# A decoder layer on one core: scaled B and C tiles laid out by batch, sums of squares in four column groups

## The reference

```python
bc = jnp.einsum('bti,oi->bto', value, W_bc).reshape(Bsz, Tlen, H, 4, N)      # H = 32 heads, N = 32 states
bc = bc / (jnp.sqrt(jnp.sum(bc * bc, axis=-1, keepdims=True)) + EPS)
Bz, Bx, Cz, Cx = (bc[..., i, :] for i in range(4))
def step(carry, inp):
    z, s = carry
    S = 1.0 / (1.0 + dt * k + dt * dt * A)
    z = S * (z - dt * A * s + dt * (Bz * u))
    s = s + dt * z + dt * (Bx * u)
    y = einsum('bhn,bhnd->bhd', Cz, z) + einsum('bhn,bhnd->bhd', Cx, s)
_, ys = jax.lax.scan(step, init, inputs_by_time)
y = (ys + skip * value) * silu(gate);  return y @ W_out.T
```

## Time and profile before

| | us |
|---|---|
| median of 3 runs | 3355.25 (3353.84 to 3386.32) |
| the profiled execution: time, and its span | 3354.0, 3352.2 |
| PE busy | 2969.5 (89%) |
| DVE busy | 2062.2 (62%) |
| ACT busy | 1303.7 (39%) |
| mean granted TensorE clock | 0.927 of full speed |

### The profile page before, as it was taken

The page is one execution under the profiler, slowest core; times in us unless marked ns, Lnnn a source line. Parts: engine busy times, 40 slices in busy tenths (PEclk is TensorE's granted clock), DMA queues, the critical chain, the costliest instruction groups (busy, mean ns, idle before and its releaser), DMA issues. The chain is left out here.

```text
span 3352.2 us, 84244 instructions
## 1 busy us (share of the span) xinstructions
PE 2969.5 (89%) x34360; PEld 2215.4 (66%) x34360; DVE 2062.2 (62%) x7109; ACT 1303.7 (39%) x2246; POOL 287.1 (9%) x227
## 2 busy tenths in 40 slices
PE   5885799999999999999999998698699389999997
PEld 2344577777787777878778776333376156888886
DVE  5445898989989999999988996455533000111110
ACT  3443345444544455444544552233221011333332
POOL 0000000000000000000000000000002710343433
PEclk9887899999999999999999998799859589999998
DMA  6556332444254324443344322200041211777777
GB/s 226 151 157 172 85 95 64 127 102 97 68 122 115 101 79 97 117 110 88 74 127 102 96 63 69 72 1 1 28 203 60 96 46 35 186 202 202 202 206 216
DMA packets 333204, 373.98 MB, mean 112 GB/s; under 512 B 62254, under 2 KB 294848, under 8 KB 328128
## 3 DMA queue, kind: packets, MB, share of 16 engines
q1 hardware_dynamic: 310400, 340.20, 36.5%
q0 software_dynamic: 22464, 28.95, 4.3%
HBM read 269.17 MB, written 104.04 MB: 111 GB/s over the span
## 5 line engine op out<-in xcount | busy, mean ns | idle before, releaser
L605 PE MATMUL ring<-valt,wbc 128*128 128x256 f32 x4096 | 943.4, 386 | 29.9 <-DMA valt<-valt_scratch 27.6
L605 PEld LDWEIGHTS ring<-valt,wbc 128*128 128x128 f32 x4096 | 772.6, 193 | 166.6 <-issue 61.1
L758 ACT COPY bc<-ring 128x512 f32<-128x512 f32 x256 | 149.6, 584 | 732.4 <-PE ring L605 732.3
L918 DVE TENSOR_TENSOR uu<-phi,coef 128x64 f32<-128x64 f32 x2048 | 359.2, 215 | 2.1
L924 DVE TENSOR_TENSOR phi<-phi,uu 128x64 f32<-128x64 f32 x2048 | 358.9, 215 | 0.0
L2023 DVE TENSOR_SCALAR f_yr<-fp_y,f_meta 128x256 f32<-128x256 f32 x124 | 54.3, 479 | 415.2 <-PE fp_y L1839 415.2
L663 PE MATMUL yp<-bc,hpad 32*32 32x64 f32 x8192 | 260.3, 289 | 3.3 <-DVE hc L1024 2.5
L663 PEld LDWEIGHTS yp<-bc,hpad 32*32 32x32 f32 x8192 | 225.3, 121 | 54.2 <-issue 54.0
L1901 ACT ACTIVATE f_hT<-fp_h,f_b 128x256 f32<-128x256 f32 x248 | 117.6, 474 | 328.2 <-PE fp_h L1830 328.2
L1839 PE MATMUL fp_y<-f_w,f_hT 128*128 128x256 f32 x992 | 230.7, 386 | 7.9
L1712 POOL DMA_INDIRECT acc_scratch<-f_yr,f_meta x124 | 192.6, 1553 | 444.3 <-DVE f_yr L2023 276.4
(11 more groups left out here) (226 smaller groups left out, 4168.6 us busy)
## 6 DMA issues: line engine op xcount, KB each, us to landing
f_w<-in_W_dram SPq DMA_DIRECT2D x128, 512.0 KB
coef<-par_scratch SPq DMA_DIRECT2D x128, 256.0 KB, 5.8
fb<-fac_scratch SPq DMA_DIRECT2D x512, 64.0 KB, 2.2
fc<-fac_scratch SPq DMA_DIRECT2D x512, 64.0 KB, 2.6
xg_scratch<-f_fill SPq DMA_DIRECT2D x16, 1032.0 KB, 17.1
f_xr<-xg_scratch SPq DMA_DIRECT2D x64, 258.0 KB
vtok_scratch<-p_vtok SPq DMA_DIRECT2D x32, 512.0 KB, 7.1
dub<-vtok_scratch SPq DMA_DIRECT2D x16, 1024.0 KB, 5.5
```

Of the source, the lines that this page charges most:

```text
L605: mm = pe.matmul(ring[:, p % 2, v * UT:(v + 1) * UT], wbc[:, k, g, first + v, :], valt[:, u % 2, k, :], start=(k == 0), stop=(k == 3))
L758: nc.scalar.copy(bc[:, gp, first:first + 2, i // 2, :], o).then_inc(bc_ready, 1)
L918: made[k] = mark(V.tensor_tensor(uu[:, k].rearrange("p i (g b) -> p i g b", b=B), phi[:, t, ::-1, k, :].rearrange("p i (g b) -> p i g b", ...
```

## The change

`sq` gets two halves, and PE adds the squares of two parts at a time: `summed` runs twice a pass in place of four times, with four program matmuls in the column groups 0 to 3 in place of two. ACT's `Square` of a part waits for the sums of two parts back, no longer for the last one. The last operations of `inputs` and `read_out` write `bc` by batch (column b*128 + i*64 + t over both halves i), reading their sources with a step of 4 elements. PE's three readers of the scaled tiles now read contiguous columns. Since the new layout of one half covers old columns of the other, both writes wait for the last of the products before them (`need(other[1])`).

```diff
-        sq = sb("sq", [P, 2, UT])
+        sq = sb("sq", [P, 2, 2, UT])
+        def batches(v):
+            return v.rearrange("p (t b) -> p b t", b=B)
+        def flat(gp, c):
+            return bc[:, gp, c].rearrange("p i t -> p (i t)")
+        def late(v):
+            return v.rearrange("p (b i t) -> p i b t", b=B, i=2)
...
-            def summed(u, gp, i):
+            def summed(u, gp, half):
...
-                for v in range(2):
-                    c = first + v
-                    mm = pe.matmul(ssp[H * c:H * c + H, 0:UT], sel[:, g, :], sq[:, v, :],
-                                   start=(i < 2), stop=(i >= 2))
+                for i in range(2):
+                    for v in range(2):
+                        c = 2 * i + v
+                        mm = pe.matmul(ssp[H * c:H * c + H, 0:UT], sel[:, g, :], sq[:, i, v, :],
+                                       start=(half == 0), stop=(half == 1))
...
                         mm = pe.transpose(kp[:, v, b * P:(b + 1) * P],
-                                          turns(bc[:, gp, v].rearrange("p i t -> p (i t)"))[:, :, b], ident[:])
+                                          flat(gp, v)[:, b * P:(b + 1) * P], ident[:])
...
                                 mm = pe.matmul(kp[L * i:L * i + L, j, b * L:(b + 1) * L],
-                                               turns(bc[r, gp, v, i, :])[:, :, b],
-                                               turns(bc[r, gp, 2 + v, i, :])[:, :, b],
+                                               flat(gp, v)[r, b * P + i * L:b * P + (i + 1) * L],
+                                               flat(gp, 2 + v)[r, b * P + i * L:b * P + (i + 1) * L],
...
                                 pe.matmul(yp[r, b * L:(b + 1) * L], hpad[r, v, i, b, :],
-                                          turns(bc[r, gp, 2 + v, i, :])[:, :, b],
+                                          flat(gp, 2 + v)[r, b * P + i * L:b * P + (i + 1) * L],
...
-                if p > 0:
-                    act.wait_ge(sums_done, p)
-                nc.scalar.activation(sq[:], o, ACT.Square).then_inc(sq_ready, 1)
+                if p >= 2:
+                    act.wait_ge(sums_done, p // 2)
+                nc.scalar.activation(sq[:, p % 2], o, ACT.Square).then_inc(sq_ready, 1)
...
                 for i, m in enumerate((m1, m2)):
-                    need(other[i])
-                    V.tensor_tensor(bc[:, gp, 0, i, :], fb[:, i, 1, :], m[:, 1, :], ALU.subtract)
-                    ins = V.tensor_tensor(bc[:, gp, 1, i, :], m[:, 0, :], fb[:, i, 0, :], ALU.subtract)
+                    need(other[1])
+                    V.tensor_tensor(late(flat(gp, 0))[:, i], batches(fb[:, i, 1, :]), batches(m[:, 1, :]), ALU.subtract)
+                    ins = V.tensor_tensor(late(flat(gp, 1))[:, i], batches(m[:, 0, :]), batches(fb[:, i, 0, :]),
+                                          ALU.subtract)
...
                 for i, m in enumerate((m1, m2)):
-                    need(other[i])
-                    ins = V.tensor_tensor(bc[:, gp, 2:4, i, :], fc[:, i], m[:], ALU.add)
+                    need(other[1])
+                    ins = V.tensor_tensor(bc[:, gp, 2:4].rearrange("p c i t -> p c (i t)")
+                                          .rearrange("p c (b i t) -> p i c b t", b=B, i=2)[:, i],
+                                          fc[:, i].rearrange("p c (t b) -> p c b t", b=B),
+                                          m[:].rearrange("p c (t b) -> p c b t", b=B), ALU.add)
```

More of the change, by code:

```diff
@@ L607, in projected @@
                 mm.then_inc(ring_full, 1)
-            def summed(u, gp, i):
+            def summed(u, gp, half):
                 n = GP * u + gp
[L612 to L615, removed]
+                g = 2 * gp + half
+                pe.wait_ge(sq_ready, 4 * n + 2 * half + 2)
+                if half == 0 and n > 0:
                     pe.wait_ge(nr_root, n)
-                for v in range(2):
-                    c = first + v
-                    mm = pe.matmul(ssp[H * c:H * c + H, 0:UT], sel[:, g, :], sq[:, v, :],
-                                   start=(i < 2), stop=(i >= 2))
+                for i in range(2):
[3 more added lines that the diff above has]
+                                       start=(half == 0), stop=(half == 1))
                 mm.then_inc(sums_done, 1)
@@ L663, in mixed_states @@
                                 pe.matmul(yp[r, b * L:(b + 1) * L], hpad[r, v, i, b, :],
-                                          turns(bc[r, gp, 2 + v, i, :])[:, :, b],
+                                          flat(gp, 2 + v)[r, b * P + i * L:b * P + (i + 1) * L],
                                           start=(b == 0 and i == 0 and v == 0), stop=False, skip_group_check=True)
                     if b == 0 and more:
-                        summed(un, gn, 3)
+                        summed(un, gn, 1)
                 for v in range(2):
@@ L699, in _ @@
                     projected(0, gp, i)
-                    if gp > 0 or i > 0:
-                        summed(0, gp - (i == 0), (i - 1) % 4)
-            summed(0, GP - 2, 3)
+                    if i == 2:
+                        summed(0, gp, 0)
+                    elif i == 0 and gp > 0:
+                        summed(0, gp - 1, 1)
+            summed(0, GP - 2, 1)
             for u in range(NU):
@@ L710, in _ @@
                         projected(un, gn, 1)
-                        summed(un, gn, 0)
                     if gp == 0 and u > 0:
@@ L716, in _ @@
                         projected(un, gn, 2)
-                        summed(un, gn, 1)
+                        summed(un, gn, 0)
                         projected(un, gn, 3)
-                        summed(un, gn, 2)
                     mixed_states(u, gp, more, un, gn)
@@ L758, in projected @@
                 nc.scalar.copy(bc[:, gp, first:first + 2, i // 2, :], o).then_inc(bc_ready, 1)
-                if p > 0:
-                    act.wait_ge(sums_done, p)
-                nc.scalar.activation(sq[:], o, ACT.Square).then_inc(sq_ready, 1)
+                if p >= 2:
+                    act.wait_ge(sums_done, p // 2)
+                nc.scalar.activation(sq[:, p % 2], o, ACT.Square).then_inc(sq_ready, 1)
             def norms(u, gp):
                 n = GP * u + gp
-                act.wait_ge(sums_done, 4 * n + 4)
+                act.wait_ge(sums_done, 2 * n + 2)
                 if n > 0:
```

## The result

The changed kernel takes 3429.41 us (median of 4 runs, 3420.26 to 3435.87); the kernel before, beside it, 3357.35. The ratio is 1.0193, 95% interval 1.0132 to 1.0255: 72 us, 2%, slower. The profiled execution took 3420.3 us, 66 more than that of before. Its last residual add starts at 2167.3 us in place of 2096.6, so 70.6 us came in up to the end of the mixer and 4 went behind it, where nothing was changed. From the first residual add to the last but one, 14 chunks take 114.3 us each, before 109.7.

A forecast was written before the change was run, and what follows sets the result against it. The prediction took DVE's own loop, not PE, as the bound: 100 us for stepped reads plus 13 for new waits, less 13, 7, 3.5 and 4, gives 85 us on 3354.0, so 3439 us; range 3385 to 3525.

The forecast's parts named there:

- What bounds the kernel: Mixer: DVE's own loop sets the chunk of 108.5 us, not PE, though PE is busy 96%.
- the two waits: DVE's waits for fb in each chunk, 2.67 and 4.81 us, made by DVE's own loop through SP and DMA.
- DVE's price: The stepped reads in inputs and read_out cost DVE 0.76 ns a column more, 1.56 us a pass, 100 us.
- the two rows that met at 1.8: PE's stepped read and ACT's stepped copy, both 1.8 ns a column, taken as the memory's price for DVE too.
- rival 2: DVE's stepped reads: penalties of both sources add, 1.52 ns a column, time 3522 us; chance 12%.
- rival 1: DVE's stepped reads are free, only the new waits add, time 3357 us; chance 12%.
- The 41 us for 1.4 ns: Low end of the forecast's own range: half the step penalty on DVE, 41 us slower, 3395 us.
- The exposed waits: New waits for the product right ahead in inputs and read_out: 0.10 us each, 13 us in all.
- What the waits swallow: DVE's fb waits hide part of its added work: 13 us in the first, 7 us in the second.
- PE's gift to DVE: Faster PE saves DVE 3.5 us of waits at the mask and 4 us at the mixer's end.
- rival 4: PE idles more, its clock stays at half for most of a chunk and PE binds, near 3600 us; chance 3%.
- Rival 3: PE sets the time after all, moving the fb waits by its sums; 3344 us, no change, 4%; 3241, faster, 3%.

The follow-up runs named there:

- tensor_only: Kernel before, with PE alone reading bc by contiguous columns (wrong column order), VectorE and sums unchanged; ratio 0.9944 to before, 18 us less.
- vector_only: Kernel before, with VectorE alone as in the changed kernel, PE and sums as before (PE reads wrong columns); ratio 1.0205 to before, 67 us more.
- sums_only: Kernel before, with only the new sums of squares in four column groups; ratio 0.9967 to before, 11 us less.
- early_factors: Kernel before, with factors(n0 + 3) moved ahead of read_out(u, 2) on VectorE; ratio 1.0003 to before.
- exposed_waits: Kernel before, with both bc writes waiting for the last product (need(other[1])), nothing else changed; ratio 1.0026 to before, 8 us at the middle.
- the trials: Kernel before, with VectorE operations of various steps and ScalarE copies added behind the mixer; 256 VectorE columns: 416 ns contiguous, 601 with one stepped source.

## Why the prediction was right, point by point

**What bounds the kernel.** Right, and shown: with PE's work 8 us a chunk smaller the time fell 0.6% (tensor_only), with DVE's 7 us larger it rose 2.0% (vector_only). Right about the two waits as they stand, but one sentence on them says less than it seems to: "PE's sums, made earlier, would move neither" holds (sums_only), but it hid that the norms were nearly as late as DVE. early_factors showed it: 49 us of waits for them come in when DVE asks sooner. A wait that a loop of DVE's makes can cover another engine's that is a little shorter.

**DVE's price** was taken as 0.76 ns a column, from PE's read and ACT's write with the same step, at 1.8. By the records it is 0.78 and 0.80. From first start to last end a call of `inputs` went from 5.04 to 5.96 us and one of `read_out` from 6.10 to 7.03; less the 0.12 us each of exposed_waits that is 0.77 and 0.79 ns a column, 1.60 us a pass, 102 us in all against 100 forecast. The size is right, the way to it partly luck: the two rows that met at 1.8 do not show one price for every engine and side. ScalarE's row is the length of a record of a write, and a write costs less in time than that length says (last section); DVE in the trials pays 0.7 to read and 0.45 to write. That the sources' penalties add, rival 2, fell by L1121 and L1123: 601 and 610 ns. That the step is free as far as 4 words, rival 1, fell by the same rows and by L1131, 609. (The point of 0.23 ns in rival 1 leaves out what the `fb` waits swallow of the price; with it 33 us are reached at 0.28. The 41 us for 1.4 ns come to 42 by the same rules. Nothing hung on either.)

**The exposed waits** were 13 us; exposed_waits gives 16 on DVE, 0.12 us for each in place of 0.10.

**Nothing else on DVE grew.** By the means over their groups it looks so: `evolve` goes from 215 to 217 ns, the other 512-column operations from 681 to 687. But these are lengths of records that overlap, and the next operation does not start later for it. A quarter of `evolve`, from its first operation to the one behind it, before and after:

```profile
1082.15 0.36 DVE L918 TENSOR_TENSOR uu<-phi,coef 128x64 f32<-128x64 f32 x2
...
1090.95 0.43 DVE L944 TENSOR_TENSOR nr<-nr,pq 128x256 f32<-128x256 f32 x1
```

```profile
1226.27 0.36 DVE L930 TENSOR_TENSOR uu<-phi,coef 128x64 f32<-128x64 f32 x2
...
1235.06 0.43 DVE L956 TENSOR_TENSOR nr<-nr,pq 128x256 f32<-128x256 f32 x1
```

8.80 and 8.79 us; summed over all 4017 starts of one operation of `evolve` right behind another, 544.2 and 544.1 us. Two 512-column operations of `read_out` start 0.60 us apart in both kernels. So the prediction missed no term here.

**What the waits swallow** is the term that was mis-sized most. The forecast was 13 + 7 = 20 us. Idle time before the `fb` group fell from 133.3 to 95.7, 38 us, nearly all of it in the first wait: 32 us over the 14 chunks, where 13 was forecast, and 2 in the second, where 7 was. The first wait did not shrink by the 0.88 us of `read_out(u, 1)`; it went, 2.3 us on average, because the loads also landed sooner. I had taken the DMA's 9.3 us, the time in one chunk, as fixed.

**PE's gift to DVE** was 3.5 us at the mask and 4 at the end. The idle time before the mask fell from 8.9 to 2.6 us, 6. The last chunk takes 65.1 us in both, though DVE's work is 3.3 us longer there: its `fb` wait is 1.5 us shorter, the one for the norms 1.1, the one for the mask 0.9. But it waits 17.1 us for the values and the outputs there, before 16.9, so the 4 us that faster products and states were to give at the end did not come. Two of PE's bursts of states there run at half clock and shorten only from 3.91 to 3.64 us.

DVE's busy time grew by 112.0 us by the page and its gaps under 0.15 us by 4.9 (28.0 against 23.1 over the whole run), together 117 or so, which is the 102 of the step and the 16 of the waits. 117 - 38 - 6 - 1 = 72 us, and the mixer's end moved by 70.6. The forecast of 85 was 113 - 20 - 7.5: its work on DVE was 4 us too small, what the waits swallow 18 too small. Another 4 us were won behind the mixer, where nothing was changed and the forecast had nothing.

**The clock**, rival 4: PE idles more and the mean granted clock of the chunk falls from 1.00 to 0.91 (over the 14 chunks 0.91 to 0.94 each), so it is low for a small part of a chunk; PE still waits 10 us a chunk for DVE, so it costs nothing that shows here. Nor would PE's contiguous states have doubled at half clock, as rival 4 took it: 3.64 us against 2.19. **Rival 3** (PE sets the time) fell by tensor_only and vector_only, though its chance was not foolish: the two loops lie within some 5 us a chunk.

## What to carry to other kernels

The engine with the larger busy share need not be the bound: look who waits for whom, and where an engine waits for a DMA, follow the DMA back to who let it start. A relayout is work for the engine with room: a step of 16 bytes in f32 cost VectorE nearly 0.8 ns a column here, and moving it from a reader with room to the engine that sets the pace loses even where the reader gains 8 us a chunk (tensor_only) for the writer's 7. If VectorE must do it, the step was cheaper here on the written side, by 1.6 us a chunk. Room won off the path is worth more with the order changed after it: the same change of SP's and ScalarE's order gave 51 us with PE's gain and 19 without. These two pairs differ in DVE's work as well, so how much of the 32 us is PE's is not shown. And judge an engine's cost from start to start: the mean length of a record can grow while no time is lost, and can hide a difference that is there.

## What was not expected of the hardware

- The penalty of a stepped access on VectorE sets in between 2 and 4 words of f32 (427 and 609 ns for 256 columns), does not add up over the operands that step by 4 (601 to 623), is about the same at 8 words (618), and doubles at 24 (798). From start to start a stepped source costs 0.7 ns a column, a stepped destination 0.45. The first part bears out the Trainium skill (Vector Engine (DVE) Microarchitecture Reference, "5.2 Measured stream behaviour on trn2"), whose granule is a pair of adjacent words: pairs at a step of 4 words run at 427 ns here. Its 2.50 ns a column for a step of 24 words agrees as well: (798 - 416) / 256 + 1.04 = 2.53 by the means, 2.49 from start to start (706 against 336 ns). A plain step of 2 words costs nothing more here either (L1129, 427 ns), though its elements are not adjacent.
- ScalarE pays the same kind of price from SBUF to SBUF, reading (L828) or writing (L831) with the step: 0.9 ns a column over the contiguous copy (L825) by the means, in the trial kernel. From start to start, two copies of each kind alone, it is 540 ns reading and 440 writing against 311, so 0.9 and 0.5 ns a column:

```profile
L828 ACT COPY dub<-pinv 128x256 f32<-128x256 f32 x2 | 1.2, 634 | 0.0
L831 ACT COPY dub<-pinv 128x256 f32<-128x256 f32 x2 | 1.1, 642 | 0.0
L825 ACT COPY dub<-pinv 128x256 f32<-128x256 f32 x2 | 0.7, 402 | 68.4 <-DVEq L1148 68.4
```

- Matmuls of 64 columns that read with a step of 16 bytes, four side by side, take the same time at either clock level: 128 of them 3.91 us at half and 4.01 at full. Contiguous ones follow the clock, 3.64 us at half and 2.19 at full. The products, which read both operands so, took 2.39 and 2.37 us and now take 2.26 at half and 1.58 at full.
